# Two feed-forward stages of a four-layer cross-attention model: order of the casts and two filler blocks in the quantised one, units on the partitions in the mixture of experts

## The reference

```python
# f0: every act_qdq needs the largest absolute value of a whole tensor
x = act_qdq(x)
up = act_qdq(x @ lpbq_dequant(w_up).T)          # 128 -> 384
gate = act_qdq(x @ lpbq_dequant(w_gate).T)
sig = fixed_qdq_u16(jax.nn.sigmoid(gate))
gate = act_qdq(gate * sig)
o = act_qdq(gate * up)
return o @ lpbq_dequant(w_down).T

# f1: 16 experts of 32 units (512 hidden units), the 4 best are used
sel_probs = jax.nn.sigmoid(jnp.einsum('btd,ed->bte', x, expert_sel))
_, sel_index = jax.lax.top_k(sel_probs, 4)
sel_val = jnp.take_along_axis(sel_probs, sel_index, axis=-1)
sel_val = sel_val / jnp.clip(sel_val.sum(-1, keepdims=True), 1e-09) * route_scale
scores_all = jax.nn.relu(jnp.einsum('btd,edh->bteh', x, keys))
values_all = jnp.einsum('bteh,ehv->btev', scores_all, values)
out = (selected * sel_val[..., None]).sum(axis=2)      # the 4 selected of values_all
```

## Time and profile before

| | us |
|---|---|
| median of 3 runs (1137.42 to 1137.57) | 1137.47 |
| the profiled execution | 1135.27 |
| its span in the trace | 1133.5 |
| PE busy | 932.4 (82%) |
| DVE busy | 833.9 (74%) |
| ACT busy | 647.1 (57%) |
| POOL busy | 464.1 (41%) |
| mean granted TensorE clock | 0.931 of full |

### The profile page before, as it was taken

How to read it: one execution, slowest core, us unless ns; L and a number is a source line. 1 busy time by engine, 2 the same in 40 slices (tenths; PEclk the granted TensorE clock), 3 DMA queues, 4 the chain that set the end, 5 groups by cost and what they waited for, 6 DMA issues and landing times.

```text
span 1133.5 us, 21105 instructions
## 1 busy us (share of the span) xinstructions
PE 932.4 (82%) x7196; PEld 630.6 (56%) x7196; DVE 833.9 (74%) x2079; ACT 647.1 (57%) x1143; POOL 464.1 (41%) x446
## 2 busy tenths in 40 slices
PE   5868810388987999899869999998988988968997
PEld 3753310374545677455436666665654546547896
DVE  6786699876887675677889999999857884623443
ACT  4424567966653345666458878785556653214553
POOL 5500000001220000544379999998311232573555
PEclk9899965699999999999989999999999997998999
DMA  8000000029000000000000000000000000124431
GB/s 296 1 1 1 1 0 0 1 75 279 2 1 1 1 1 2 1 1 2 2 1 1 1 0 0 0 0 1 1 1 1 2 2 1 39 104 115 115 104 33
DMA packets 24234, 33.77 MB, mean 30 GB/s; under 512 B 3484, under 2 KB 20389, under 8 KB 23888
## 3 DMA queue, kind: packets, MB, share of 16 engines
q1 hardware_dynamic: 20720, 26.20, 7.6%
q0 software_dynamic: 3424, 6.38, 1.7%
HBM read 18.34 MB, written 15.98 MB: 30 GB/s over the span
## 4 chain that ended last, share of the span: by engine, by line
PE 35%; DVE 28%; issue 8%; ACT 5%; POOL 2%; DVEq 1%; DMA 0%; POOLq 0%; ACTq 0%
DVE big L864 7%; DVE hq L859 7%; PE psum L620 5%; PE psum L2570 5%; PE psum L1619 3%; DVE big L2220 2%; PE psum L2586 2%; ACT psum L2069 2%; PE psum L574 2%; DVE big L868 2%; PE psum L1636 2%; POOL rows L2433 1%; DVE psum L1871 1%; DVE tmp L1859 1%; DVE psum L1859 1%
## 5 line engine op out<-in xcount | busy, mean ns | idle before, releaser
L859 DVE TENSOR_REDUCE hq<-psum 128x16 f32<-128x1024 f32 x96 | 114.2, 1220 | 62.9 <-PE psum L574 36.2
L2143 POOL TENSOR_TENSOR big<-big 128x512 f32<-128x512 f32 x128 | 128.6, 1042 | 7.0 <-ACT big L1899 7.0
L2069 ACT ACTIVATE psum<-big,tmp 128x512 f32<-128x512 f32 x128 | 84.9, 686 | 19.6 <-DVE big L2220 16.9
L2220 DVE SCALAR_TENSOR_TENSOR big<-big,tmp,psum 128x512 f32<-128x512 f32 x128 | 90.4, 744 | 4.5 <-ACT psum L2069 1.3
L749 ACT ACTIVATE big<-psum 128x1024 f32<-128x1024 f32 x64 | 62.0, 1021 | 49.1 <-PE psum L604 49.1
L864 DVE RECIPROCAL big<-psum 128x256 f32<-128x256 f32 x48 | 84.0, 1749 | 4.9 <-PE psum L620 4.7
L2762 DVE SCALAR_TENSOR_TENSOR big<-psum,big 128x128 f32<-128x128 f32 x118 | 36.1, 348 | 69.6 <-issue 46.9
L484 POOL TENSOR_TENSOR big<-big,w_const 128x256 f32<-128x256 f32 x32 | 23.9, 749 | 144.5 <-PE psum L620 137.3
L1533 PE MATMUL psum<-f_downT,tmp 128*128 128x128 f32 x192 | 24.9, 294 | 68.0 <-DVE tmp L1413 68.0
L2153 POOL TENSOR_TENSOR big<-big 128x1024 f32<-128x1024 f32 x32 | 75.2, 2361 | 11.7 <-DVE big L2220 11.7
L2443 POOL DMA_INDIRECT out<-big x59 | 58.0, 983 | 50.2 <-issue 29.5
(11 more groups left out here) (341 smaller groups left out, 2626.3 us busy)
## 6 DMA issues: line engine op xcount, KB each, us to landing
rows<-pad SPq DMA_DIRECT2D x1, 7670.0 KB, 33.8
big<-rows SPq DMA_DIRECT2D x59, 130.0 KB, 2.2
tmp<-in_pack_f SPq DMA_DIRECT2D x1, 2050.5 KB, 9.5
w_f<-in_pack_f SPq DMA_DIRECT2D x1, 1280.0 KB, 12.2
tmp<-in_pack_once SPq DMA_DIRECT2D x1, 960.0 KB, 7.1
out<-big POOLq DMA_INDIRECT x59
X<-in_x SPq DMA_DIRECT2D x1, 768.0 KB, 5.5
w_a<-in_pack_a SPq DMA_DIRECT2D x3, 256.0 KB, 8.0
```

The costliest lines, as they stand in the source:

```text
L859: dve.tensor_reduce(nm, psum[:, 1 + 2 * t:3 + 2 * t, :].rearrange("p c (r l k) -> p (c r) l k", r=2, k=SK), AX.X, ALU.max, negate=True).th ...
L2069: act.activation(bank(EX_BANK + h % 2), ssum[t][:, h * 512:(h + 1) * 512], ACT.Exp, bias=shift2[:, t * NH2 + h:t * NH2 + h + 1]).then_inc( ...
L2143: ins = pool.tensor_tensor(ssum[t][:, h * 512:(h + 1) * 512].rearrange("p (i j) -> p i j", i=ROWS2), st[:, 0, h, 0:ROWS2].unsqueeze(2).to_ ...
L2220: dve.scalar_tensor_tensor(out=ew[t][:, blk], in0=ssum[t][:, blk], scalar=best2[:, t, h, 7:8], in1=bank(EX_BANK + h % 2), op0=ALU.is_ge, o ...
```

## The change

There are three parts.

1. In `f0_dve` the cast of group g+2 moves from behind the search of GATE g to directly behind the levels of group g+2, in front of both searches.
2. In `f0_pe` two blocks of matmuls are added whose results nothing reads: four fp32 matmuls of 128x256 as soon as the first maximum is found, in front of the first turn, and seven once `f0_d2` says that DVE is through the products of all eight groups, in front of the down projection.
3. In f1 the 512 units of a group lie on the partitions, in four blocks c of 128 units x 512 tokens, in place of four tiles of 128 tokens x 512 units. `keys(g, c)` has the keys as weights and `hT` as the moving side. The result needs no transposing, so `tr` and its ACT copies go. But the gates must now lie as units x tokens: DVE splits the fp32 gates into three bf16 parts that add up to them (five more operations in `f1_gates`), PE turns them (`parts(g)`, four matmuls of 48x128 into bank 0), ACT copies them (`take_parts`, 48x512), PE spreads them over the units with a 0/1 matrix `esel16` (`spread(g, c)`, one bf16 matmul of 48 rows and 512 columns for each block, banks 4 and 5) and ACT copies each result to `gx1` (`take_spread`). `hidden(g, c)` multiplies the relu of `keys(g, c)` by `gx1`. `val(g, t)` needs all four blocks, so it runs within the body of group g+1, and the residual of group g two bodies later. The last group's `val` stands between the first query products of a2, and its residual behind the four `a2.mx`. `gate1`'s users in DVE move too: the gates of g+1 stand in front of `hidden(g, 2)`. `esel16` comes with the pack of constants "once" (960 to 1216 KB) and is cast by one operation in `rows_finish_dve`.

The diff without the counts of semaphores that only follow from it:

```diff
@@ f0_dve
                 if g + 2 < N_GROUPS:
                     token_levels(g + 2)
+                    tokens(g + 2)
                 dve.wait_ge(S("f0_gu"), 2 * g + 1)
                 absmax(1, GATE, g)
-                if g + 2 < N_GROUPS:
-                    tokens(g + 2)
                 dve.wait_ge(S("f0_gu"), 2 * g + 2)
                 absmax(2, UP, g)
@@ f0_pe
+            def fill(n, to):
+                for _ in range(n):
+                    pe.matmul(bank(to)[:, 0:256], W["a1_wk"], ctx_keys(0, 4), start=True, stop=True)
+            pe.wait_ge(S("f0_pmax"), 1)
+            fill(4, 0)
             turn(pe, "f0", 0, 0)
...
+            pe.wait_ge(S("f0_d2"), N_GROUPS)
+            fill(7, 7)
             for g in range(N_GROUPS):
                 pe.wait_ge(S("f0_oq"), g + 1)
@@ f1_gates, behind the last gate operation
+            dve.tensor_copy(gs1[:, :, 0, :], ga).then_inc(S("f1_g"), 1)
+            dve.tensor_tensor(re, ga, gs1[:, :, 0, :], ALU.subtract).then_inc(S("f1_g"), 1)
+            dve.tensor_copy(gs1[:, :, 1, :], re).then_inc(S("f1_g"), 1)
+            dve.tensor_tensor(re, re, gs1[:, :, 1, :], ALU.subtract).then_inc(S("f1_g"), 1)
+            dve.tensor_copy(gs1[:, :, 2, :], re).then_inc(S("f1_g"), 1)
@@ f1_pe
+            def parts(g):
+                pe.wait_ge(S("f1_g"), 17 * g + 17)
+                for t in range(GT):
+                    ins = pe.matmul(bank(0)[0:3 * MOE1_E, t * P:(t + 1) * P], gs1[:, t].rearrange("p i e -> p (i e)"),
+                                    ident16[:, :], start=True, stop=True)
+                ins.then_inc(S("f1_lg"), 1)
+            def spread(g, c):
+                if c == 0:
+                    pe.wait_ge(S("f1_ex"), 2 * g + 2)
+                if 4 * g + c >= 2:
+                    pe.wait_ge(S("f1_gx"), 4 * g + c - 1)
+                pe.matmul(bank(4 + c % 2), esel16[0:3 * MOE1_E, c * P:(c + 1) * P], gT1[g % 2][0:3 * MOE1_E, :],
+                          start=True, stop=True).then_inc(S("f1_gx_ps"), 1)
+            def keys(g, c):
+                if 4 * g + c >= 2:
+                    pe.wait_ge(S("f1_hidT"), 4 * g + c - 1)
+                pe.matmul(bank(2 + c % 2), W["f1_keys"][:, c * P:(c + 1) * P], hT[:, g % 2, :], start=True, stop=True)
+                    .then_inc(S("f1_h_ps"), 1)
...
-                tr(0)
-                keys(2)
-                tr(1)
...
-                val(0)
-                keys(3)
-                tr(2)
-                val(1)
...
+                spread(g, 0)
+                if not last: turn(pe, s, g + 1, ...)
+                keys(g, 0)
+                spread(g, 1)
+                keys(g, 1)
+                if not last: f1_logits(pe, g + 1, ...)
+                if g: val(g - 1, 0); val(g - 1, 1)
+                spread(g, 2)
+                keys(g, 2)
+                if g in (5, 6): a2.V(2 * g - 9, 6)
+                if g: val(g - 1, 2)
+                if not last: parts(g + 1)
+                spread(g, 3)
+                keys(g, 3)
+                if g: val(g - 1, 3)
@@ f1_act
-                    act.activation(hidT1[t % 2], bank(4 + t % 2), ACT.Copy).then_inc(S("f1_hidT"), 1)
+                act.activation(gT1[g % 2][0:3 * MOE1_E, :], bank(0)[0:3 * MOE1_E, :], ACT.Copy)   # take_parts
+                act.activation(gx1[c % 2], bank(4 + c % 2), ACT.Copy).then_inc(S("f1_gx"), 1)      # take_spread
@@ f1_dve
+            def hidden(g, c):
+                dve.wait_ge(S("f1_h_ps"), 4 * g + c + 1)
+                dve.wait_ge(S("f1_gx"), 4 * g + c + 1)
+                dve.scalar_tensor_tensor(out=hidT1[g % 2][:, c * GN:(c + 1) * GN], in0=bank(2 + c % 2), scalar=0.0,
+                                         in1=gx1[c % 2], op0=ALU.max, op1=ALU.mult).then_inc(S("f1_hidT"), 1)
```

More of the change, by code:

```diff
@@ L1561, in build @@
         gate1 = f1.take(GT * MOE1_E)
-        hid1 = [f1.take(512) for _ in range(2)]
-        hidT1 = [f1.take(512) for _ in range(2)]
+        gs1 = f1.take(GT * 3 * MOE1_E, BF16).rearrange("p (t i e) -> p t i e", t=GT, i=3)
+        rest1 = f1.take(GT * MOE1_E)
+        gT1 = [f1.take(GN, BF16) for _ in range(2)]
+        gx1 = [f1.take(GN) for _ in range(2)]
+        hidT1 = heads["a2"].pt
         def f1_logits(pe, g, j):
@@ L1641, in body @@
+            def body(g, last):
                 if g == 1:
@@ L1673, in body @@
                     a2.V(2 * g - 9, 6)
[L1674 to L1683 removed]
+                if g:
+                    val(g - 1, 2)
+                if not last:
+                    parts(g + 1)
+                else:
+                    a2.Q(0)
+                spread(g, 3)
+                keys(g, 3)
+                if g:
+                    val(g - 1, 3)
+            parts(0)
+            for g in range(N_GROUPS):
+                body(g, g == N_GROUPS - 1)
+            a2.Q(1)
+            val(N_GROUPS - 1, 0)
+            a2.T(1)
+            val(N_GROUPS - 1, 1)
             a2.MX(0, 0)
[L1685 removed]
+            val(N_GROUPS - 1, 2)
             a2.MX(0, 1)
             a2.Q(2)
+            val(N_GROUPS - 1, 3)
             a2.MX(1, 0)
@@ new lines, in take_spread, with body @@
+            def take_spread(g, c):
+                act.wait_ge(S("f1_gx_ps"), 4 * g + c + 1)
+                if 4 * g + c >= 2:
+                    act.wait_ge(S("f1_hidT"), 4 * g + c - 1)
+                act.activation(gx1[c % 2], bank(4 + c % 2), ACT.Copy).then_inc(S("f1_gx"), 1)
+            def body(g, last):
+                take_spread(g, 0)
+                if g in (5, 6):
+                    a2.values(2 * g - 10, 6)
+                if not last:
+                    take_turned(act, "f1", g + 1, (g + 1) % 2)
+                else:
+                    normalise_act(act, "a2", 1, 1)
+                take_spread(g, 1)
+                if not last:
+                    f1_exps(act, g + 1, (g + 1) % 2)
+                else:
+                    take_turned(act, "a2", 0, 0)
+                take_spread(g, 2)
+                if g + 2 < N_GROUPS:
+                    normalise_act(act, "f1", g + 2, g % 2, int(4 * (g + 2) >= EARLY))
+                if not last:
+                    take_parts(g + 1)
+                else:
+                    a2.takeQ(0)
+                take_spread(g, 3)
@@ L1762, in body @@
                     ln_var_dve(dve, "a2", 0)
+                hidden(g, 0)
                 if g == 6:
                     ln_rstd_dve(dve, "a2", 0)
+                hidden(g, 1)
+                if g < N_GROUPS - 1:
+                    f1_gates(dve, g + 1, (g + 1) % 2)
                 hidden(g, 2)
                 hidden(g, 3)
-                if not (fixed and g == N_GROUPS - 1):
-                    f1_gates(dve, g + 1, 1 - j)
                 if g == 0:
@@ L1783, in f1_dve @@
             for g in range(N_GROUPS):
[L1784 to L1785 removed]
+                body(g)
+            res(N_GROUPS - 2)
             for b in range(2):
```

138 lines of the change are left out of this document (52 added, 86 removed).

## The result

The changed kernel takes 1144.54 us in the median of 4 runs (1142.61 to 1145.5), the kernel before beside it 1137.52 (1137.42 to 1138.3). The ratio is 1.0058, with a 95% interval of 1.0041 to 1.0076: slower by 6.6 us, where 1128.2 was forecast. The profiled execution took 1144.44 us with a span of 1142.6, so 9.1 us more span than before.

The account below looks back on a forecast made before the run. PE and DVE were taken to share the chain of waits, neither alone bounding it. −8.0 −0.7 −1.1 +0.5 = −9.3 on the profiled 1135.27 gave 1126.0, plus 2.2 for the median 1128.2; eight in ten 1121.9 to 1134.0.

Parts of the forecast that it names:

- Part 1, −8.0: f0 loop: with casts directly behind the levels, six PE waits of 1.34 us go, −8.0 us.
- Part 2, −0.7 and −1.1: Fillers raise PE's clock earlier: −0.7 us at f0's first turn, −1.1 at the down projection.
- The full ends: Largest gains of the two filler blocks, f0's start −1.7 us and down projection −1.6, which the skill's advice would give.
- Net of part 3 … = +0.5: f1 rewrite: PE work −4.3, waits that go −4.7 and −0.7, waits that come +9.9, small gaps +0.3, together +0.5 us.
- the prediction's own sign of being wrong: f1 becoming more than 5 us shorter or longer, from its first keys to the first scores of a2.
- Work off PE, −0.54 a group: f1 on PE: transposes −1.72, four spreads +0.92, parts +0.26, so −0.54 us a group, −4.3 in all.
- a bound of 6.4 on the spreads: f1: spreads at 0.43 us, half the fp32 product, in place of 0.23 would be 6.4 us worse.
- its range of −4.3 to +4.5: f1 net, in us, with both ends of the unknown prices and every hidden gap.
- The clock: Rival: new waits in f1's groups 0 and 4 drop PE's clock, two stretches at 1.7, +3.4 us, 1131.6; chance 0.20.
- Waits that come, +9.9: f1 and a2's keys: PE waits 3.0 us at group 0's parts, 1.4 later, 4.9 at a2's keys, 0.6 at a turn.
- the eight-in-ten range: Whole kernel: 1121.9 us (full saving and both fillers in full) to 1134.0 (clock and half the casts' shortfall).
- The slower rival: f1: dearer split steps on DVE make the gate chain the bound, 1.7 us a group, +13.6, 1141.8; chance 0.07.

Follow-up runs that it names:

- e16: Kernel before with the moved casts and the seven fillers ahead of the down projection, without the four ahead of the first turn: 1127.49 us, ratio 0.9921.
- e2: Kernel before with only the fillers, four ahead of the first turn and seven ahead of the down projection: ratio 0.9965.
- e12: Changed kernel with each spread issued twice in a row into the same bank: 0.54 us for the pair, 0.21 for each added product.
- e8: Changed kernel with the spreads in pairs and the parts behind the keys of block 3: ratio 1.0037.
- e7: Changed kernel with eight fp32 filler matmuls in f1's idle stretches, around the first parts and ahead of group 1's: ratio 0.9974.
- e14: The kernel of e10, timed, all three parts with f1 fillers and the f2 loop at 1241: 1130.26 us, ratio 0.9937.
- e10: The kernel of e7 with 72 semaphore instructions at the head of DVE's program, f2 loop at 1241: 1127.55 us in one run.
- e4: Kernel before with 56 semaphore instructions at the head of DVE's program, f2 loop at 1169 in place of 1113: ratio 1.0057.
- e13: Changed kernel with only 72 semaphore instructions at the head of DVE's program, f2 loop at 1241: 1135.32 us, ratio 0.9973.
- e1: Kernel before with only the casts moved directly behind the levels: ratio 0.992.
- e15: As e14 but with the spreads in pairs: 1134.61 us, ratio 0.9975.

## Why the prediction was wrong, point by point

**Part 1, −8.0.** Right: 6 waits of 1.34 are gone, with rounds of 5.59. From 86 to 141 us the changed kernel gains 9.0 with the first block of fillers, e16 8.0 without it.

**Part 2, −0.7 and −1.1.** Right within 1 us. The first block started 1.6 late and delayed the turn by some 1.1, and gave it back with the clock; net it gave 0 to 1.0 (e2, e16). The second gave 1.5. The full ends that the prediction set beside its own values (−1.7 and −1.6) came close to true for the second block and not for the first.

**Part 3, the step that failed: "Net of part 3 … = +0.5".** DVE measured +9.9 (from 349 to 475). On PE, from the start of a1's last product to the first L600 or L601 of a2, it is +9.5 (352.72 to 460.73 before, 343.01 to 460.52 after), and the terms below are set against this. By the prediction's own sign of being wrong, more than 5 us from f1's first keys, it is +7.8 to that L600 or L601 (357.30 and 349.27 are the first keys). Its terms:
- *Work off PE, −0.54 a group.* The product's price was right (e12: 0.21), but PE alternates between bf16 and fp32, and each island of bf16 costs 0.3 more (rows above, e8, e12: the weights of the next product don't load ahead across the switch). Four islands a group make +1.2, so 8 × 1.2 = +9.6, and PE's work in a group grew instead of shrinking. The logits of groups 2 and 3 lie 379.51 − 367.15 = 12.36 apart, where 11.5 was forecast and the kernel before has 386.00 − 374.09 = 11.91. The prediction had named a bound of 6.4 on the spreads, for a dearer product, and then left it out of its range of −4.3 to +4.5.
- *The clock.* It was a rival with +3.4. 15.4 us of work ran at half clock in place of 2.9: at most +6.2. e7 wins back 5.9 with no half clock at all, where the kernel before has 1.5 of such loss itself: +4.4. The rival was the right mechanism with the wrong waits: one stretch of 20.4 us at the start of f1 in place of two short ones, while the wait in group 4 (1.75) passed at full clock. The Trainium skill ("TensorE: Matmul & The Clock Gate", section "Why this matters for your kernels") says that idle gaps between bursts of matmuls bring the clock back to half and that TensorE should be warmed up with matmuls first. The second agrees with e7, 1.00 where the changed kernel has 0.50. The first agrees only in part: the fall at 343.8 comes ahead of the 2.80, and behind the same 2.84 in a2 the clock falls in e14 and not in e10.
- *Waits that come, +9.9.* They measured 1.42 at parts(1), 0.68 ahead of the first spread, and 0.55, 0.55, 1.75 and 0.55 at a2's keys: 5.5. The gates were never late from group 1 on. A slower PE covered what DVE had to do, so this term was too high for a reason that the other two give.
0.5 + 9.6 + 4.4 − 4.4 = 10.1, where 9.5 was measured; the 0.6 isn't split, since some switches of groups 0 and 1 lie in waits.

Three readings of the prediction are off without changing much: the waits at a2's keys add up to 4.8, not 4.9; the low end of the eight-in-ten range comes to 1122.4 by its own terms, not 1121.9; and the idle stretch at the end of f0 lasts 3.13 by its row, not 2.6 (the clock falls 2.5 us into it).

**A term that was missing: the place of a loop in an engine's program.** Not one sentence of the sum was about f2. Its loop on DVE costs 5.8 us more since 56 instructions stand in front of it (e4 shows it on the kernel before, e13 takes it away from the changed one). I had counted the added instructions only as work.

**Another: half-clock stretches in unedited stages**, +4.0 in a2. The sum had no term for them. That the change brings them isn't shown: e10 and e14 are one program, with and without such a stretch, and e1, e2 and e4 have them without part 3. All four executions of the changed kernel lie at 1142.61 or above, so the loss as a whole is no single execution's. How much of it these stretches are on average stays open. So forecast −9.3 on the profiled execution, measured +9.1 in span: the 18.4 between them are 9.4 in f1, 5.8 in f2, 4.0 in a2 and −0.8 in all the rest.

The slower rival, the gate chain at 0.45 and more a step, was wrong: the five split operations took 0.19 to 0.23 each. The time came out on its side of the forecast by other ways.

## What to carry to other kernels

When bf16 products are put between fp32 ones, price the switches too: 0.3 us for an island of one or two bf16 products here. Keeping pieces of one kind together saves switches, but e8 and e15 gained no time by it, as other waits grew. After adding instructions ahead of a loop in the program, compare the first instruction of its body in both traces: a wait for nothing that grows there can come from the loop's place, and idle instructions at the head of that engine's program can take it away. Before a half-clock stretch in an unedited stage is put down to an edit, look at a second execution of the same kernel. Where two edits of one change lie in different stages, run them apart: here parts 1 and 2 alone (1125.82 us, 0.9905) beat both kernels.

## What the runs showed that I had not expected

- A loop of 285 instructions on DVE waits 0.4 us or 2.9 to 3.1 us at each jump back, by where it starts: 0.4 at 1113, 1241 and 1369, 2.9 to 3.1 at 1169 and 1177.
- A bf16 product among fp32 ones costs 0.3 us beyond its own 0.21: the fp32 products in front of it and behind it 0.96 each in place of 0.86, its own slot 0.31. The weights of a product load ahead of it between fp32 products (389.53 for 389.64), but not across the switch.
- Two executions of one program on one chip (e10, e14) keep and lose the full clock behind the same wait of 2.84.
- Eight added fp32 products in f1's idle stretches, their results unused, made f1 5.9 us shorter, in a stage where PE is the busiest engine. The half-clock start of f1 that they remove stands in all four traces with part 3 whose PE order in f1 has neither fillers nor pairs (17.1 to 20.5 us).
